# Score levels inside 32 positions computed in 32-wide blocks: compact 128x32 tiles instead of 128x128 score tiles

## What is computed

```python
def step(S, qkva):
    q_t, k_t, v_t, a_t = qkva
    S = a_t[..., None] * S + k_t[..., None] * v_t[:, :, None, :]
    o_t = jnp.einsum('bhkv,bhk->bhv', S, q_t)
    return (S, o_t)
```

## Time and profile before

| | |
|---|---|
| median of 3 runs | 2142.69 us (2139.69 to 2145.41) |
| profiled execution: span | 2138.3 us |
| attention part / feed-forward part of the span | about 1604 us / 534 us |
| PE, PEld, DVE, ACT, POOL busy | 94%, 79%, 80%, 51%, 43% |
| mean granted TensorE clock | 0.988 |
| one loop iteration (four slots) | 98.1 us: 25.8, 25.0, 23.2, 24.2 us |

### The profile page before, as it was taken

How to read it: one execution, slowest core, us unless ns; L and a number is a source line. 1 busy time by engine, 2 the same in 40 slices (tenths; PEclk the granted TensorE clock), 3 DMA queues, 4 the chain that set the end, 5 groups by cost and what they waited for, 6 DMA issues and landing times.

```text
span 2138.3 us, 49851 instructions
## 1 busy us (share of the span) xinstructions
PE 2005.2 (94%) x16903; PEld 1690.3 (79%) x16903; DVE 1712.6 (80%) x3516; ACT 1095.9 (51%) x2352; POOL 922.1 (43%) x729
## 2 busy tenths in 40 slices
PE   7999999999999999999999999999988999999997
PEld 5888888888888888888888888888875666666664
DVE  4988888788878787888788787878885777777876
ACT  5555445455445455545455444555534555555554
POOL 5444444344434344444434444434422444444443
PEclk8999999999999999999999999999999999999999
DMA  6000000000000000000000000000000000000000
GB/s 182 2 6 7 2 6 2 7 1 7 1 7 2 7 6 2 6 2 7 2 7 2 7 1 7 2 7 6 2 1 11 21 10 20 20 10 20 20 10 15
DMA packets 28482, 24.53 MB, mean 11 GB/s; under 512 B 1928, under 2 KB 23696, under 8 KB 28304
## 3 DMA queue, kind: packets, MB, share of 16 engines
q1 hardware_dynamic: 28304, 21.77, 3.3%
HBM read 13.38 MB, written 4.19 MB: 8 GB/s over the span
## 4 chain that ended last, share of the span: by engine, by line
PE 51%; issue 21%; DVE 17%; POOL 9%; ACT 1%; DVEq 1%; POOLq 0%; DMA 0%; SPq 0%; ACTq 0%
PE bank L599 15%; DVE k_sb L1211 7%; PE bank L589 6%; PE bank L517 4%; POOL wq_lo L485 4%; PE bank L519 4%; PE bank L518 4%; POOL wk_lo L485 4%; PE bank L606 4%; PE bank L634 3%; PE bank L577 3%; PE bank L648 2%; PE bank L622 2%; DVE at_sb L1224 2%; DVE qq_sb L1172 2%
## 5 line engine op out<-in xcount | busy, mean ns | idle before, releaser
L441 POOL TENSOR_TENSOR sq_lo<-sq_sb,sq_hi 128x512 bf16<-128x512 f32 x256 | 348.7, 1362 | 581.0 <-ACT sq_hi L947 581.0
L1211 DVE TENSOR_TENSOR qq_sb<-qq_sb,tot_sb 128x512 f32<-128x512 f32 (+1 forms) x384 | 304.2, 792 | 195.6 <-PE bank L599 187.0
L599 PE MATMUL bank<-qq_sb,k_sb 128*128 128x64 f32 x3072 | 376.9, 276 | 12.9 <-DVE k_sb L1211 10.1
L599 PEld LDWEIGHTS bank<-qq_sb,k_sb 128*128 128x128 f32 x3072 | 364.8, 193 | 27.0 <-DVE k_sb L1211 16.3
L1211 DVE TENSOR_TENSOR k_sb<-k_sb,tot_sb 128x512 f32<-128x512 f32 (+1 forms) x384 | 298.6, 778 | 1.3 <-PE bank L606 1.3
L446 POOL TENSOR_TENSOR rn_sb<-ss_sb,expo 128x8 f32<-128x8 f32 x128 | 213.9, 1671 | 194.3 <-DVE ss_sb L1258 194.0
L1224 DVE COPY_PREDICATED at_sb<-mask_half,bank 128x512 f32<-128x512 int32 (+1 forms) x320 | 220.3, 730 | 0.0
L969 ACT ACTIVATE v_sb<-bank,rn_sb 128x128 f32<-128x128 f32 x512 | 139.0, 383 | 118.5 <-PE bank L519 107.8
L485 POOL TENSOR_TENSOR wq_lo<-v_sb,wq_hi 128x512 fp32r<-128x512 f32 x80 | 103.8, 1298 | 146.5 <-ACT wq_hi L1107 146.5
L485 POOL TENSOR_TENSOR wk_lo<-v_sb,wk_hi 128x512 fp32r<-128x512 f32 x80 | 104.3, 1304 | 133.3 <-ACT wk_hi L1107 133.3
L991 ACT ACTIVATE at_sb<-bank 32x256 f32<-32x256 f32 x64 | 23.8, 373 | 262.1 <-PE bank L606 262.1
(11 more groups left out here) (199 smaller groups left out, 4885.4 us busy)
## 6 DMA issues: line engine op xcount, KB each, us to landing
x_nat<-in_L_attn_x_dram SPq DMA_DIRECT2D x16, 256.0 KB, 2.7
x_nat<-x_all SPq DMA_DIRECT2D x16, 256.0 KB, 2.3
out_dram<-k_sb SPq DMA_DIRECT2D x16, 256.0 KB, 2.3
ew_raw<-in_L_ffn_exp_w_dram SPq DMA_DIRECT2D x3, 512.0 KB, 5.6
qq_sb<-in_L_attn_Wq_dram SPq DMA_DIRECT2D x1, 512.0 KB, 4.7
qq_sb<-in_L_attn_Wk_dram SPq DMA_DIRECT2D x1, 512.0 KB, 5.8
k_sb<-in_L_attn_Wg_dram SPq DMA_DIRECT2D x1, 512.0 KB, 6.6
k_sb<-in_L_attn_Wv_dram SPq DMA_DIRECT2D x1, 512.0 KB
```

The lines of the kernel that those rows point to most:

```text
L441: nc.gpsimd.tensor_tensor(sq_lo[:, n, :], sq_sb[:, n % 2, :], sq_hi[:, n, :], ALU.subtract).then_inc(sq_done, 1)
L599: mm = nc.tensor.matmul(bank[:, g * 64:(g + 1) * 64], k_sb[par][:, lo:lo + C], halves(qd_sb[par][:, lo:lo + C], HALF[j])[:, :, 1, :], star ...
L1211: return nc.vector.tensor_tensor(view, view, by, ALU.mult)
```

## The change

Levels 0 to 5 only have scores inside aligned blocks of 32 positions. They are now computed block by block (SB = 32, NB = 4 blocks in a chunk, HB = 16): each matmul has the 32 columns of k of one block stationary and writes 32 partitions of the bank. The result of a level is 128x(8 tiles x 16 columns) instead of 128x512 elements. DVE collects the levels in a compact tile `diag_sb` of 128x(8x32). `spread_diagonal` on ACT copies its four groups of 32 partitions to their places on the diagonal of `at_sb`, which GpSimd zeroes once at the start. Levels 1 and 2 become one step, so a slot has 7 steps (qk_full) and 6 evacuations by DVE (sc_evac) instead of 8 and 8. The diff, cut to its core:

```diff
+    STEPS = 7
+    EVACS = 6
+    SB = 32
+    NB = C // SB
+    HB = SB // 2
+        mask_sub = sb("mask_sub", [128, 4, HB])
+        diag_sb = sb("diag_sb", [128, G, SB])
-        def bank_of_step(j):
-            return sc[(j + 1) % 2]
+        ORDER = (0, 1, 3, 4, 5, 6, 7)
+        WIDTH = {0: HB, 1: SB, 3: HB, 4: HB, 5: HB, 6: SB, 7: 2 * SB}
+        def columns(par, j):
+            return sc[(par * STEPS + ORDER.index(j) + 1) % 2][:, 0:G * WIDTH[j]]
...
         pool_setup(pool)
+            for i in range(2):
+                nc.gpsimd.memset(at_sb[i][:, :, :], 0.0).then_inc(at_zero, 1)
...
-                    nc.tensor.matmul(bank[:, :], ones_wide[:, :], e_sb[:, :], start=True, stop=True).then_inc(qk_full, 1)
+                    for n in range(NB):
+                        moving = e_sb[:, :].rearrange("p (g n t) -> p g n t", n=NB, t=HB)[:, :, n, :]
+                        mm = nc.tensor.matmul(out[n * SB:(n + 1) * SB, :].rearrange("p (g t) -> p g t", t=HB),
+                                              ones_wide[:, 0:SB], moving, start=True, stop=True)
...
+                if j == 1:
+                    await_count(pe, sc_act, P * 3)
+                    pe.wait_ge(q1_done, 3 * (P + 1))
+                    for g in range(G):
+                        for n in range(NB):
+                            lo = g * C + n * SB
+                            moving = qq_sb[par][:, :, lo:lo + SB].rearrange("p w (n two m) -> p w n two m", two=2, m=2)[:, :, :, 1, :]
+                            mm = nc.tensor.matmul(out[n * SB:(n + 1) * SB, g * SB:(g + 1) * SB].rearrange("p (w n m) -> p w n m", w=2, m=2),
+                                                  k_sb[par][:, lo:lo + SB], moving, start=True, stop=True)
...
-                    if j < 6:
-                        mm = nc.tensor.matmul(bank[:, g * 64:(g + 1) * 64], k_sb[par][:, lo:lo + C],
-                                              halves(qd_sb[par][:, lo:lo + C], HALF[j])[:, :, 1, :], start=True, stop=True)
+                    for n in range(NB if j < 6 else C // (2 * m)):
+                        left = g * C + (n * SB if j < 6 else 2 * m * n)
+                        if j < 6:
+                            mm = nc.tensor.matmul(out[n * SB:(n + 1) * SB, g * HB:(g + 1) * HB], k_sb[par][:, left:left + SB],
+                                                  halves(qd_sb[par][:, left:left + SB], m)[:, :, 1, :], start=True, stop=True)
...
-                pe.wait_ge(sc_evac, (P + 1) * 8)
+                pe.wait_ge(at_diag, (P + 1) * NB)
...
+            def spread_diagonal(par, P):
+                act.wait_ge(sc_evac, (P + 1) * EVACS)
+                if isinstance(P, int) and P == 0:
+                    act.wait_ge(at_zero, 2)
+                await_count(act, av_done, (P - 1) * HP)
+                for n in range(NB):
+                    rows = slice(n * SB, (n + 1) * SB)
+                    nc.scalar.activation(at_sb[par][rows, :, rows], diag_sb[rows, :, :], ACT.Copy).then_inc(at_diag, 1)
...
                         take_gate(1 - par, P + 1)
+                    spread_diagonal(par, P)
                     take_scores_32(par, P)
...
-                dst = at_sb[par][:, first_group:first_group + groups, :]\
-                    .rearrange("p g (n two m) -> p g n two m", two=2, m=m)[:, :, :, 1, :]
+                dst = diag_sb[:, :, :].rearrange("p g (n two m) -> p g n two m", two=2, m=m)[:, :, :, 1, :]
...
             def take_own(par, P):
-                await_count(dve, av_done, (P - 1) * HP)
+                await_count(dve, at_diag, P * NB)
```

More of the change, by code:

```diff
@@ L76, in gated_linear_attention_and_moe_block @@
     L2_EPS = 1e-12
-    STEPS = 8
+    STEPS = 7
+    EVACS = 6
     SS = 32
-    HALF = {j: 2 ** (j - 1) for j in range(2, STEPS)}
+    SB = 32
+    NB = C // SB
+    HB = SB // 2
+    HALF = {j: 2 ** (j - 1) for j in range(2, 8)}
     ctx = ExitStack()
@@ L233, in gated_linear_attention_and_moe_block @@
         sc_act = sem("sc_act")
+        at_zero = sem("at_zero")
+        at_diag = sem("at_diag")
         kt_full = sem("kt_full")
@@ L570, in scores @@
             def scores(par, P, j):
-                bank = bank_of_step(j)
+                out = columns(par, j)
                 if j == 0:
@@ L603, in scores @@
[L603 to L608, removed]
+                    for n in range(NB if j < 6 else C // (2 * m)):
[3 more added lines that the diff above has]
+                                                  halves(qd_sb[par][:, left:left + SB], m)[:, :, 1, :], start=True, stop=True)
+                        else:
+                            mm = nc.tensor.matmul(out[2 * m * n:2 * m * n + m, g * m:(g + 1) * m],
+                                                  k_sb[par][:, left:left + m], qd_sb[par][:, left + m:left + 2 * m],
+                                                  start=True, stop=True)
@@ L909, in _ @@
             pe.wait_ge(e_lo, 3)
-            pe.wait_ge(const_dve, 2)
+            pe.wait_ge(const_dve, 5)
             ffn(0, first=True)
@@ L1321, in _ @@
             clamp_sums(0, 1)
-            dve.wait_ge(const_dve, 1)
+            dve.wait_ge(const_dve, 5)
             for h in range(HP):
@@ L1338, in body @@
                     qk = P * STEPS
-                    for h in range(HP):
-                        dve.wait_ge(qk_full, qk + 2 + h)
-                        keep_masked(at_sb[par][:, h * NC:(h + 1) * NC, 1::2], merged(h)[:, :, 0, :], mask_odd[:, :], NC)
-                    dve.wait_ge(sc_evac, P * 8 + 3)
+                    dve.wait_ge(qk_full, qk + 2)
+                    keep_masked(diag_sb[:, :, 1::2], merged(par)[:, :, 0, :], mask_odd[:, :])
                     grow(par, 2, "q").then_inc(q_up, 1)
+                    dve.wait_ge(sc_evac, P * EVACS + 2)
                     grow(par, 2, "k").then_inc(k_up, 1)
-                    for h in range(HP):
-                        keep_level(par, 2, h * NC, NC, merged(h)[:, :, 1, :])
+                    keep_level(2, merged(par)[:, :, 1, :])
                     for j in range(3, 7):
```

57 lines of the change are left out of this document (31 added, 26 removed).

## The result

The changed kernel takes 2015.33 us (median of 4 runs, 2013.13 to 2016.19), the kernel before 2141.19 us (2137.98 to 2145.41): a ratio of 0.941, 95% interval 0.9395 to 0.9425. That is 126 us less, where 2005 us and so 138 us were forecast, inside both ranges of the prediction. The profiled execution has a span of 2013.3 us and a mean granted clock of 0.96, where it was 0.988.

A forecast was written before the change was run, and what follows sets the result against it. PE was taken to set the pace nearly everywhere: 1.95 + 0.4 = 2.35 us a slot, times 64, 150 us, less 14, gives 136 us and 2005 us. Own range 1970 to 2055; 8 in 10, 1925 to 2100.

The forecast's parts named there:

- A level thus costs 1.16 + 0.13 + 0.11 = 1.40 us: PE, levels 1 to 5: 64 narrow instructions at twice level 6's row, plus shape changes behind and ahead; was about 1.81 us.
- rival (a): PE levels: four places run side by side, a level costs 0.9 us, 3.4 us a slot saved, 1939 us; chance 0.17.
- Level 0: PE, level 0 as 8 instructions of 128 moving columns: 0.6 us, a saving of 0.3 us a slot, bounds 0 and 0.45.
- PE's saving: PE per slot: 1.65 us from levels 1 to 5 plus 0.3 from level 0, together 1.95 us.
- Rival (b): PE levels: a narrow instruction costs 25 ns, a level 1.84 us, nothing won on levels 1 to 5, 2112 us; chance 0.15.
- (c): PE gets narrow instructions too slowly, 35 ns for load and matmul, a level 2.48 us, 2284 us; chance 0.08.
- PE still sets the pace: After the change, per slot: DVE falls from 20.4 to 17.4 us of work, PE from 23.3 to 21.4 us.
- 15 turns: PE's loop turns: 4 us of level 0's saving not won, and 8 us for commoner half-clock stretches.
- DVE's part: DVE's smaller copies, 0.19 us each for 128 elements, save 3.0 us of DVE work a slot; busy about 1520 us.
- the 0.4 us a slot: PE's waits for DVE, 0.6 us a slot before, shrink by 0.4 us because DVE's copies get shorter.
- ACT's part: ACT's four added copies, 0.37 us each, 1.5 us a slot, hidden in ACT's waiting, cost nothing; ACT busy 95 us more.
- The two alarms: Signs the forecast is wrong: mean granted clock well under 0.98, or long unexplained waits in front of narrow levels.

The follow-up runs named there:

- experiment 2: Changed kernel with tile and block loops exchanged in levels 1 to 5, so 16 narrow instructions in a row write one place: 2123.05 us, ratio 0.9915.
- experiment 1: Changed kernel with PE's loop body holding two sequences instead of one, seven turns fewer: 1965.1 us, ratio 0.9162.
- experiment 6: Kernel before the change with PE's loop body holding two sequences instead of one: 2117.36 us, ratio 0.9885.
- experiment 8: Changed kernel with PE's loop body holding seven sequences, twelve turns fewer: 1921.06 us, ratio 0.8974.
- experiment 5: Changed kernel with DVE's state recurrence moved ahead of level 4's copy: 1968.32 us, ratio 0.9189.
- experiment 11: Kernel before the change with DVE's state recurrence moved ahead of level 4's copy: 2116.54 us, ratio 0.9881.
- Experiment 12: Changed kernel with two useless 128x128 matmuls on PE in the wait for the state: 1990.99 us, ratio 0.9295.
- experiment 10: Changed kernel with seven-sequence PE loop body and early state recurrence, plus first sums of squares and their clamp moved behind level 4: 2050.98 us, ratio 0.9574.
- experiment 4: Changed kernel with wide matmuls again in levels 0 to 5, DVE's copies still compact, scores wrong: 2127.06 us, ratio 0.9924.
- experiment 3: Kernel before with only levels 1 to 5 as narrow matmuls; level 0, DVE and ACT as before: 2030.53 us, ratio 0.9476.

## Why the prediction came out right, and which step of it failed

The forecast stood at 2005 us and the kernel takes 2015, but this nearness is two errors that nearly cancel.

**The cost of a level was mis-sized.** "A level thus costs 1.16 + 0.13 + 0.11 = 1.40 us" is the step that failed: it is 0.70 us from start to start, with 0.04 us of shape change behind it where I could read it. I had seen that level 6 alternates between two places and the new levels between four, and still doubled level 6's time. That four places at once take half was rival (a) with 0.17; experiment 2 shows its mechanism directly, since the same instructions with one place at a time cost 1.82 us. Level 0 was forecast well, 0.34 us for 0.3. PE's saving was thus 4.4 us a slot, not 1.95. Rival (b), 25 ns for each narrow instruction, is refuted by 11 ns a pair, and so is (c), a supply too slow inside the levels, except behind a loop turn, where levels 1 and 2 do stop for instructions. The rule of the Trainium skill, "TensorE: Matmul & The Clock Gate", section "Wait — 56ns, not 53.3ns?", that matmuls never start closer than about 25 ns, doesn't hold in this trace for neighbours in different places; pairs in one place stand 28 ns apart (experiment 2).

**"PE still sets the pace" fell with it.** With a slot of 18.9 us on PE (23.3 less 4.4) DVE and POOL hold it in places. Of the 282 us that the faster levels give, 126 arrived. Two takers were shown. The 13 loop turns took 55 us more than before (experiments 1, 6 and 8), where I had counted 15 turns and put 12 us (4 for level 0, 8 for the clock). The wait for `s_sb` with the low clock behind it took about 22 us (experiments 5 and 11). Experiment 12 prices that low clock at 20 to 25 us; it is most likely the same loss seen again, and is not added. That leaves some 80 us without a price. In the trace stand waits for `sq_lo` (28.7 us) and `res` (18.2 us), levels that wait for `grow`, and DVE's slower pieces beside POOL; experiment 10 tried to take the first of these away and failed, so where the 80 us went is not shown. Rival (a)'s 1939 us with these corrections, + (55 - 12) + 22, is 2004 us. That comes near, but its 3.4 us a slot were an estimate, so it is no proof.

**DVE's part** was right in its small numbers: 0.20 us a copy (0.19 forecast). The copies' busy time fell by 197 us in all (192 forecast). DVE's whole fell only to 1595 us and not to 1520: `grow` of k rose from 824 ns in the trace before to 1075, while that of q fell from 842 to 696, 34 us more together, and the products of gates (the 1.05 us row above is one) took 44 us more. On the time DVE's part is worth about 16 us by experiment 4; the 0.4 us a slot, 26 us, were somewhat too much.

**ACT's part** was right: busy 98.6 us more (95 forecast), 0.41 us a copy, and no row in which PE waits for them.

**What was to be seen afterwards.** Right: 12288 instructions on the new line, and hardly any wait before level 7. Wrong: the level's 1.2 us, and the slots of 23.4, 22.5, 20.8 and 21.9 us, which are 26.5, 21.9, 22.3 and 21.5. The two alarms that I had named at the end, a mean clock well under 0.98 and waits for instructions at narrow levels, both came true (0.96, and L607's 20.0 us): they were the other half of the cancelling.

## What to carry to other kernels

When a small matmul leaves parts of the array free, price it by how many different places its neighbours in the queue use, not by its size. When one engine becomes much faster, expect the gain to be handed to what was hidden under it: look at the loop turn first, then at each in-order queue, and ask what stands behind the instruction that will wait. And an idle microsecond of PE can cost more than itself, so its place is worth as much as its length.

## What the runs showed of the hardware that I had not expected

- Pairs of load and matmul with 32 stationary columns: 28 ns a pair with one place (64 pairs, 16 moving columns), 20 with two (32 pairs, 32 moving), 11 with four in turn (64 pairs, 16 moving).
- A turn of PE's hardware loop costs 3.5 us in the kernel before and 7.6 to 7.8 us in the changed one; there PE stops a second time, 1.64 us in the turn shown, within levels 1 and 2. With 29191 matmuls in the program but level 0 and DVE as before (experiment 3) there was no second stop.
- After 1.36 us of idle time PE ran for 3.41 us at a granted clock of 0.50; with 0.72 us of idle time after two useless matmuls at the same place it did not, and the kernel was 25 us faster.
- A DVE multiply of 128x512 from SBUF took 0.69 us, and 1.66 us while POOL ran its own tensor operation.
